# An output bias that moves from a vector sum into two one-row products of TensorE

## The reference

```python
msgs  = x[src]                                    # (100000, 512)
neigh = segment_sum(msgs, dst, 6250)
rst   = (1 + eps[0]) * x + neigh
h     = maximum(rst @ W1 + b1, 0)                 # W1 (512, 1024)
h     = h @ W2 + b2                               # W2 (1024, 512)
out   = layernorm(x + (h + x), eps=1e-5)          # over the 512 features
```

## Time and profile before

| | |
|---|---|
| median of three runs | 1056.1 us |
| the profiled execution | 1057.84 us |
| its span (first to last instruction) | 1056.3 us |
| granted TensorE clock, mean share | 0.992 |
| PE busy | 981.2 us (93%), 5540 matmul records |
| POOL busy | 779.5 us (74%), and 240.4 us before gathers put down to "issue" |
| DVE busy | 433.9 us (41%) |
| ACT busy | 171.0 us (16%) |
| DMA | 244.40 MB, mean 231 GB/s |

### The profile page before, as it was taken

How to read it: one execution, slowest core, us unless ns; L and a number is a source line. 1 busy time by engine, 2 the same in 40 slices (tenths; PEclk the granted TensorE clock), 3 DMA queues, 4 the chain that set the end, 5 groups by cost and what they waited for, 6 DMA issues and landing times.

```text
span 1056.3 us, 16350 instructions
## 1 busy us (share of the span) xinstructions
PE 981.2 (93%) x5540; PEld 565.7 (54%) x5540; DVE 433.9 (41%) x1038; ACT 171.0 (16%) x312; POOL 779.5 (74%) x819
## 2 busy tenths in 40 slices
PE   1459999999999999999999999999999999999997
PEld 1116565555555555655555555555555555555555
DVE  4533434344334344343344334334334334433433
ACT  1112111111111111111111111111111111111111
POOL 7777777777777777777777777777777777777770
PEclk9979999999999999999999999999999999999999
DMA  6887777877877778778777777777877877777770
GB/s 205 289 285 229 238 235 228 246 232 235 244 230 238 243 229 241 238 228 242 236 227 238 236 230 231 244 227 228 247 231 227 246 232 230 240 237 226 231 228 28
DMA packets 85904, 244.40 MB, mean 231 GB/s; under 512 B 17319, under 2 KB 20110, under 8 KB 85878
## 3 DMA queue, kind: packets, MB, share of 16 engines
q0 software_dynamic: 64544, 210.95, 67.1%
q1 hardware_dynamic: 21334, 33.10, 9.5%
HBM read 230.37 MB, written 13.62 MB: 231 GB/s over the span
## 4 chain that ended last, share of the span: by engine, by line
POOL 41%; PE 40%; issue 14%; DMA 3%; DVE 1%; POOLq 0%; ACT 0%; SPq 0%; DVEq 0%
POOL raw L460 41%; PE hp L1136 13%; PE y L1152 12%; PE acc L1171 11%; DMA raw<-in_x_dram,idx 1%; PE turned L1122 1%; DMA win<-in_dst_dram 1%; PE turned L1112 1%; PE hturned L1122 1%; PE tables L1050 1%; POOL shared L508 0%; POOL pair_shared L486 0%; POOLq L286 0%; DVE late L917 0%; DVE raw L754 0%
## 5 line engine op out<-in xcount | busy, mean ns | idle before, releaser
L460 POOL DMA_INDIRECT raw<-in_x_dram,idx x800 | 767.5, 959 | 245.1 <-issue 240.4
L1171 PE MATMUL acc<-raw,onehot 128*32 128x512 f32 x2200 | 300.9, 607 | 28.0 <-DMA raw<-in_x_dram,idx 25.4
L1152 PE MATMUL y<-w_hi,hT_hi 128*125 128x512 f32 x400 | 166.6, 417 | 2.9 <-DVE hT_lo L922 2.9
L1136 PE MATMUL hp<-w_hi,rstT_lo 128*125 128x512 f32 x400 | 162.9, 407 | 0.0
L1136 PE MATMUL hp<-w_hi,rstT_hi 128*125 128x512 f32 x400 | 162.2, 406 | 0.0
L1152 PE MATMUL y<-w_lo,hT_hi 128*125 128x512 f32 x400 | 161.8, 404 | 0.0
L1152 PE MATMUL y<-w_hi,hT_lo 128*125 128x512 f32 x400 | 158.5, 396 | 0.0
L1136 PE MATMUL hp<-w_lo,rstT_hi 128*125 128x512 f32 x400 | 157.7, 394 | 0.0
L917 DVE TENSOR_TENSOR late<-hp,b1b 125x512 f32<-125x512 f32 x100 | 69.1, 691 | 181.7 <-PE hp L1136 181.7
L1171 PEld LDWEIGHTS acc<-raw,onehot 128*32 128x32 f32 x2200 | 57.0, 109 | 127.2 <-issue 81.8
L1152 PEld LDWEIGHTS y<-w_hi,hT_hi 128*125 128x125 f32 x400 | 74.1, 185 | 62.5 <-issue 44.0
(11 more groups left out here) (116 smaller groups left out, 606.9 us busy)
## 6 DMA issues: line engine op xcount, KB each, us to landing
raw<-in_x_dram,idx POOLq DMA_INDIRECT x800, 3.7
xt<-in_x_dram SPq DMA_DIRECT2D x50, 224.0 KB
out_dram<-late SPq DMA_DIRECT2D x50, 224.0 KB
late<-in_L_gnn_W_dram SPq DMA_DIRECT2D x7, 512.0 KB, 7.7
xt<-in_x_dram SPq DMA_DIRECT2D x50, 26.0 KB
out_dram<-late SPq DMA_DIRECT2D x50, 26.0 KB
win<-pairs SPq DMA_DIRECT2D x51, 16.0 KB, 3.4
rst<-in_L_gnn_W_dram SPq DMA_DIRECT2D x1, 512.0 KB, 13.5
```

Source lines behind the costliest of these rows:

```text
L460: pool.indirect_dma_start(out=raw[:, i, k, :], out_offset=None, in_=table[:, :], in_offset=bass.IndirectOffsetOnAxis(ap=idx[:, slot, k:k + ...
L1136: mm = pe.matmul(hp[n][0:TN, :], rstT[b][:, c, :], w1[a][:, c, n * D:(n + 1) * D], start=(c == 0 and a + b == 0), stop=(c == TC - 1 and a ...
L1152: mm = pe.matmul(y[0:TN, :], hT[a][:, j, :], w2[b][:, j, :], start=(j == 0 and a + b == 0), stop=(j == HC - 1 and a == 1))
L1171: return pe.matmul(acc[i][q * QN:(q + 1) * QN, :], hot, rows, start=((q, k) == of_q[0]), stop=((q, k) == of_q[-1]))
```

## The change

b2 is loaded as one row. Once, ACT rounds it to fp32r (the high part) and copies a row of 125 ones, and DVE subtracts to get the low part. In each tile layer 2 begins with two products of one row each, ones by high part and ones by low part, which write b2 into all rows of `y`; the 24 products of layer 2 then add to it. `double_x` is gone, and `residuals` does z = 2x + y in one operation. PE's program has the two products between its wait for `s_z` and its wait for `s_hlo`.

```diff
-        b2b = sb("b2b", [P, D], F32)
+        b2row = sb("b2row", [1, D], F32)
+        b2r = [sb(f"b2r_{s}", [1, D], F32R) for s in ("hi", "lo")]
+        one_row = sb("one_row", [1, TN], F32R)
...
-                    sp.dma_start(b2b[:, :], b2.partition_broadcast(P)).then_inc(s_b2, 16)
+                    sp.dma_start(b2row[:, :], b2.rearrange("(a n) -> a n", a=1)).then_inc(s_b2, 16)
...
                     window_f32(4, 0, 1)
+                    act.wait_ge(s_b2, 16)
+                    act.activation(b2r[0][:, :], b2row[:, :], ACT.Copy).then_inc(s_b2hi, 1)
+                    act.activation(one_row[:, :], all_ones[0:1, 0:TN], ACT.Copy).then_inc(s_b2hi, 1)
                     hidden(0)
...
-            def double_x(F, slot):
-                dve.wait_ge(s_rst, F + 1)
-                if type(F) is int and F == 0:
-                    dve.wait_ge(s_b2, 16)
-                dve.scalar_tensor_tensor(out=xt[0:TN, slot, :], in0=xt[0:TN, slot, :], scalar=2.0,
-                                         in1=b2b[0:TN, :], op0=ALU.mult, op1=ALU.add).then_inc(s_double, 1)
-
             def residuals(F, f, slot, stores):
-                dve.wait_ge(s_double, F + 1)
...
-                dve.tensor_tensor(z[0:TN, f, :], xt[0:TN, slot, :], y[0:TN, :], ALU.add).then_inc(s_z, 1)
+                dve.scalar_tensor_tensor(out=z[0:TN, f, :], in0=xt[0:TN, slot, :], scalar=2.0, in1=y[0:TN, :],
+                                         op0=ALU.mult, op1=ALU.add).then_inc(s_z, 1)
...
                     one_hots_shared(3, 3)
+                    dve.wait_ge(s_b2hi, 1)
+                    dve.tensor_tensor(b2r[1][:, :], b2row[:, :], b2r[0][:, :].bitcast(F32),
+                                      ALU.subtract).then_inc(s_b2lo, 1)
                     add_bias(0, 0)
...
+                if first:
+                    pe.wait_ge(s_b2hi, 2)
+                    pe.wait_ge(s_b2lo, 1)
+                for s in range(2):
+                    pe.matmul(y[0:TN, :], one_row[0:1, :], b2r[s][0:1, :], start=(s == 0), stop=False)
                 for j in range(HC):
                     if j % TC == 0:
                         pe.wait_ge(s_hlo, HALVES * T + j // TC + 1)
                     for a, b in ((0, 0), (0, 1), (1, 0)):
                         mm = pe.matmul(y[0:TN, :], hT[a][:, j, :], w2[b][:, j, :],
-                                       start=(j == 0 and a + b == 0), stop=(j == HC - 1 and a == 1))
+                                       start=False, stop=(j == HC - 1 and a == 1))
```

More of the change, by code:

```diff
@@ L256, in build @@
         s_y = sem("s_y")
-        s_double = sem("s_double")
+        s_b2hi = sem("s_b2hi")
+        s_b2lo = sem("s_b2lo")
         s_z = sem("s_z")
@@ L991, in tile @@
                     rst_lo(0)
-                    double_x(0, 0)
                     make_rst(1, 1, 1, 0, True)
@@ L1003, in tile @@
                     rst_lo(1)
-                    double_x(1, 1)
                     make_rst(2, 0, 2, 0, False)
@@ L1011, in tile @@
                     rst_lo(T - 1)
-                    double_x(T - 1, (slot + 3) % 4)
                     one_hots(T + 1, 1 - i, (slot + 1) % 4, False)
@@ L1033, in _ @@
             rst_lo(TILES - 1)
-            double_x(TILES - 1, (TILES - 1) % 4)
             norm(TILES - 2, 0, (TILES - 2) % 4, 32 * last)
```

## The result

The changed kernel takes 1071.89 us (median of six runs, 1070.27 to 1074.28) against 1058.38 us for the kernel before (six runs, 1055.86 to 1065.25). The ratio is 1.0122, with a 95% interval of 1.0102 to 1.0143. The forecast was 1054, range 1050 to 1062. It was wrong: the medians lie 13.5 us apart, and the interval is clear of no change.

What follows compares the result with a forecast made beforehand. POOL's gathers set the end, PE having 20.9 us of slack. POOL's path -3 + 0.4 + 0.1 = -2.5 us, PE's -5 to 0; taken together -2, so 1056.1 - 2 = 1054 us, range 1050 to 1062.

Steps and rivals of the forecast that it cites:

- slack of PE: PE in the second half, where it waits for POOL's gathers: 20.9 us of slack.
- The point of decision: The pair's price on PE from which it decides the time: 20.9 / 48 = 0.435 us a tile.
- The price of the pair: Two one-row products ahead of layer 2 on PE: 0.33 to 0.43 us a tile taken, over 48 tiles.
- the upper bound of 0.65: Highest price for the pair on PE, from isolated one-row products plus a step: 0.65 us a tile, nothing hidden.
- The third rival: Each pair empties PE's array: 0.68 us a tile at one end (1068), 1.03 at both (1085); chance 0.10.
- `double_x` and the gathers: Without `double_x` on DVE, POOL's gathers lose delays: 3 us taken, between none and 4.6 us.
- The long gathers are gone: Sign that the forecast holds, on POOL: gathers above 1.2 us gone, 1.255 us a step or less.
- The forecast of 1054: Whole kernel: 1056.1 - 2 = 1054 us; with the case of POOL keeping its delays, chance 0.62.
- The load of b2: SP's transfer of 2 KB instead of 256 KB: PE may start up to 1.1 us earlier, zero for the end.
- The sums of the first tiles: Sign of being wrong: the start of these sums moves by more than a microsecond.

Runs made afterwards that it cites:

- full_pair: The changed kernel with its two bias products over 128 equal rows, weights 1/128, instead of one row; ratio 0.9956, 1055.48 us.
- beside_tables: The changed kernel with the one-row pair moved behind the 16-row transposes of the index tables in tiles 2 to 49; ratio 0.9986, 1062.47 us.
- four_rows: The changed kernel with four one-row products a tile instead of two, the further two of weight zero; ratio 1.0292, 1095.43 us.
- rows64: The changed kernel with its two bias products over 64 rows, weights 1/64, instead of one row; ratio 1.0098, 1073.87 us.
- double_two: full_one with an instruction reading two SBUF tensors (2x plus zeros) back in the place of `double_x`; ratio 1.0001, 1059.70 us.
- no_pair: The changed kernel without the bias products, their load and preparation, `double_x` still gone; ratio 0.9948, 1055.74 us.
- pair_only: The kernel before, `double_x` kept, with two one-row products of zeros added ahead of layer 2; ratio 1.0102, 1072.22 us.
- full_one: The changed kernel with both parts of b2 in one 128-row product a tile, 64 rows each, weights 1/64; ratio 0.9954, 1056.53 us.
- full_one_again: The same kernel as full_one, run again beside double_two; ratio 0.9966, 1056.01 us.

## Why the prediction was wrong, point by point

- **Who bounds, and the slack of PE.** Right, and the figure held: with 0.73 us a tile, 48 x 0.73 - 20.9 = 14.1 us, and the spans differ by 1071.1 - 1056.3 = 14.8. The point of decision, 0.435 us a tile, separates full_pair (0.33, faster) from the kernels with a step (0.73, slower). beside_tables (0.54) lies just past it: 48 x 0.54 - 20.9 = +5.0 for PE alone, and its profiled span, 1061.0 us, is 4.7 above the one before. On its own chip the kernel before took 1064.02 us, so there the same path was no loss (ratio 0.9986).
- **The price of the pair.** This is the step that failed: "I take 0.33 to 0.43, because the 16-row transposes ... cost just 0.22 us for two ... and leave nothing else behind". The products themselves cost what was reckoned, 0.33 us with the filled wait (full_pair). The steps on and off the few-row side add 0.39, and the 0.73 in all lie above even the upper bound of 0.65. The rows chosen could not show this. The 16-row transposes follow the sums of 32 columns, and after the last of those sums the next product starts 0.52 us later in the trace before, whether it has 16, 125 or 128 rows; their own step on was hidden in that. The step off stood in the rows, unread. The first product of 128 rows starts 0.22 us after the first of the two transposes; in beside_tables the one-row pair, on the same side as they, starts 0.14 us after it. So 0.08 us of the 0.22 were a step. The 0.33 us behind it says nothing of rows: full_pair's first product behind transposes of 125 rows takes 0.32 to its successor too (410.78, 411.10).
- **The third rival** had the mechanism, with a chance of 0.10. Its price was 0.68 us a tile for one end and 1.03 for both; it came as 0.70 to 0.73 for both. The steps are 0.19 us on entry and 0.20 on exit, for 1, 32 and 64 rows alike. The Trainium skill (TensorEngine Tiling (Array Packing), Key Properties) says that "Mode switching requires drain", and the traces agree with it in that a cost stands at each change and nowhere inside a sequence (four_rows); that the array is emptied there, they don't show. The same page (Available Configurations) lists 64-row and 32-row tilings and none between 64 and 128, which agrees with rows64. It should have weighed more than two rows that weren't placed to answer it.
- **`double_x` and the gathers.** Right in size, 3 us reckoned and 3.7 measured by double_two, and in that `double_x` delays gathers. In the changed kernel it is worth nothing, since POOL is no longer the bound; no_pair and full_pair show it as a gain. One sign of it came true for another reason. The long gathers are gone from the changed kernel, but also from pair_only, which keeps `double_x`. Gathers after 80 us (ns min/median/max, first and last start), before, after, pair_only:

```profile
L460 POOL DMA_INDIRECT raw<-in_x_dram,idx x753: 942/946/1465, 80.2 to 1026.8; - x189
```

```profile
L463 POOL DMA_INDIRECT raw<-in_x_dram,idx x753: 941/946/1143, 79.2 to 1027.1; - x189
```

```profile
L463 POOL DMA_INDIRECT raw<-in_x_dram,idx x753: 942/947/1146, 79.6 to 1027.8; - x189
```

So at PE's slower pace `double_x` made no gather long, as it made none long before the change between 206 and 451 us. How the pace decides which gathers it meets isn't shown.
- **The forecast of 1054** was a fall of 2 us, and full_pair has one: its ratio of 0.9956 is 4.7 us less, between 1.8 and 7.5. The reasoning was right for a pair of full height.
- **The load of b2.** The sums of the first tiles moved by more than the microsecond allowed: they start at 63.72 us, not at 67.03. As a sign of being wrong this was too sharp: full_one and full_one_again are the same kernel, and start these sums at 63.96 and at 69.98 us. Layer 1 of tile 0 begins where it did, see below.

## What to carry to other kernels

A product of few rows between products of 128 rows is not a small one: on TensorE it pays for two changes of height, 0.39 us a visit here, as much as 1.7 products of 512 columns. Fill it up to full height instead (n equal rows with weights 1/n, or both parts of a number in one product), or place it beside work that is on the few-row side already. A price for a new kind of instruction is to be read from rows with the same neighbours on both sides, and slack is to be reckoned as a point of decision for the price, since past that point the whole of it is on the path.

full_pair and full_one are faster than both kernels, by half a per cent against the kernel before: 0.9956 (0.9929 to 0.9983) and, over two sets of runs, 0.9954 (0.9930 to 0.9977) and 0.9966 (0.9949 to 0.9984) of the kernel before.

## What was not expected of the hardware

In the changed kernel's trace the first layer 1 ran in part on a lower clock. Busy time by stretch (us, then busy us and records of PE, PEld, DVE, ACT, POOL, then the granted clock, the DMA share and GB/s), after, and behind it before:

```profile
72.00:78.00 6.00, 6.00 (x29) 3.28 (x25) 2.65 (x8) 0.00 (x0) 4.48 (x6) 0.68 0.67 190
```

```profile
72.00:78.00 6.00, 6.00 (x41) 3.14 (x44) 5.88 (x11) 2.29 (x4) 4.78 (x5) 1.00 0.63 190
```

PE got through 29 products and not 41. The sums had come 3.3 us earlier, but PE then waited 1.79 us for gathers, and its clock was still at the 1.2 GHz level for part of this stretch, where before it was at the 2.4 GHz level throughout. That took back what the early start had won. Whether the smaller load of b2 brought the early start isn't shown: full_pair, which loads all 256 KB, starts the same sums at 65.43 us, no_pair, which loads nothing, at 65.16, and the two traces of full_one lie 6 us apart. PE comes out of this stretch 0.85 us later than before (the next sums start at 77.83 us, before at 76.98), little beside 48 x 0.73 us.
